# Attention block of eight cores: the odd cores' sums of exponentials by ones matmuls of 32 columns in groups of four, and VectorE's part handed over five steps into the next block

## The reference

```python
q = (x @ Wq).reshape(B, T, H, Dh)            # k and v alike; x here is layernorm(x)
scores = jnp.einsum('bthd,bshd->bhts', q, k)
scores = scores * jnp.tril(jnp.ones((T, T)))  # masked scores are 0, not minus infinity
attn = jax.nn.softmax(scores / T ** 0.5, axis=-1)
out = jnp.einsum('bhts,bshd->bthd', attn, v).reshape(B, T, H * Dh) @ Wo
x = x + layernorm(out)
g = jnp.einsum('th,ih->ti', xf, gate_w) * gate_s   # xf = layernorm(x), INTER = 5632
u = jnp.einsum('th,ih->ti', xf, up_w) * up_s
out = jnp.einsum('ti,hi->th', jax.nn.silu(g) * u, down_w) * down_s
x = x + layernorm(out)
```

## Time and profile before

| | |
|---|---|
| median of 3 runs | 3783.23 us (3782.91 to 4057.18) |
| profiled execution | 3785.3 us, span 3783.8 us on core 7, the slowest |
| odd cores' spans (1, 3, 5, 7) | 3778.8, 3769.3, 3779.7, 3783.8 us |
| even cores' spans (0, 2, 4, 6) | 3709.4, 3714.5, 3705.3, 3709.6 us |
| core 7 busy: TensorE, VectorE, ScalarE | 3685.2, 1424.9, 1158.5 us |
| core 7, span | 3783.8 us = phase A to 1000, B to 1958, W to 2167, C to the end |

### The profile page before, as it was taken

How to read it: one execution, slowest core, us unless ns; L and a number is a source line. 1 busy time by engine, 2 the same in 40 slices (tenths; PEclk the granted TensorE clock), 3 DMA queues, 4 the chain that set the end, 5 groups by cost and what they waited for, 6 DMA issues and landing times.

```text
span 3783.8 us, 50455 instructions; the slowest of 8 cores (3705.3 to 3783.8 us)
## 1 busy us (share of the span) xinstructions
PE 3685.2 (97%) x19252; PEld 1840.7 (49%) x19252; DVE 1424.9 (38%) x1860; ACT 1158.5 (31%) x1511; POOL 173.1 (5%) x235
## 2 busy tenths in 40 slices
PE   6999889999999999999999999999999999999998
PEld 3554444444454555545544444444444456645654
DVE  4641001101389999999976611102111121111112
ACT  2330000000288888888863310000010001101100
POOL 0000000000010000100000000000200001002000
PEclk9999989999999999999999999999999999999999
DMA  7534767798544335353036564554745547666665
GB/s 197 173 123 105 117 124 129 125 134 131 84 62 94 92 78 112 77 106 82 29 134 222 176 209 156 183 173 111 239 156 184 178 145 273 232 212 222 235 201 178
DMA packets 140788, 566.57 MB, mean 150 GB/s; under 512 B 38016, under 2 KB 83200, under 8 KB 111360
## 3 DMA queue, kind: packets, MB, share of 16 engines
q1 hardware_dynamic: 59520, 381.70, 29.6%
q0 software_dynamic: 11440, 125.83, 20.5%
q10 hardware_dynamic: 69584, 55.72, 4.9%
HBM read 595.73 MB, written 147.85 MB: 197 GB/s over the span
## 4 chain that ended last, share of the span: by engine, by line
PE 94%; ACT 2%; DMA 1%; issue 1%; ACTq 1%; DVE 1%; another core or an unknown queue 0%; DVEq 0%; POOL 0%; POOLq 0%; SPq 0%
PE ps L335 93%; ACT pt L369 1%; PE ps L340 1%; ACTq L331 1%; DMA xst<-x 0%; DMA indf<-ind 0%; DVE bna L361 0%; DVE zad L358 0%; ACT rz L369 0%; DMA kscr<-stg 0%; ACT xy L369 0%; DVE xy L360 0%; ACT zst L368 0%; DVE xn L359 0%
## 5 line engine op out<-in xcount | busy, mean ns | idle before, releaser
L335 PE MATMUL ps<-zt,slab 128*128 128x512 bf16 (+1 forms) x5632 | 1069.0, 353 | 6.2 <-DVE xy L360 6.2
L335 PEld LDWEIGHTS ps<-zt,slab 128*128 128x128 bf16 x5632 | 551.7, 98 | 522.4 <-issue 9.9
L369 ACT ACTIVATE pt<-ps 128x1024 bf16<-128x1024 f32 (+2 forms) x752 | 724.9, 981 | 132.9 <-PE ps L335 103.5
L358 DVE TENSOR_TENSOR zad<-zad,pt 128x1024 f32<-128x1024 f32 (+5 forms) x640 | 614.6, 975 | 59.5 <-POOL pt L364 2.9
L335 PE MATMUL ps<-dp,hall 128*128 128x512 bf16 x2332 | 504.0, 379 | 0.0
L360 DVE SCALAR_TENSOR_TENSOR hall<-ps,us_sb,sg 128x512 bf16<-128x512 f32 (+1 forms) x176 | 120.3, 684 | 902.6 <-PE ps L335 902.6
L335 PE MATMUL ps<-qh,kh 128*128 128x512 bf16 (+1 forms) x1760 | 432.4, 339 | 9.8 <-ACT qh L368 5.8
L335 PE MATMUL ps<-pt,vh 128*128 128x512 bf16 (+1 forms) x1760 | 432.3, 339 | 1.8 <-ACT pt L369 1.1
L369 ACT ACTIVATE sg<-ps,gs_sb 128x512 f32<-128x512 f32 (+1 forms) x176 | 111.2, 635 | 878.1 <-PE ps L335 878.0
L357 DVE CAST stg<-ps 128x512 bf16<-128x512 f32 (+1 forms) x136 | 89.7, 660 | 743.0 <-PE ps L335 707.4
L335 PEld LDWEIGHTS ps<-dp,hall 128*128 128x128 bf16 x2332 | 228.2, 98 | 274.9
(11 more groups left out here) (80 smaller groups left out, 1904.8 us busy)
## 6 DMA issues: line engine op xcount, KB each, us to landing
slab<-gwc SPq DMA_DIRECT2D x44, 2048.0 KB, 8.7
slab<-uwc SPq DMA_DIRECT2D x44, 2048.0 KB, 9.5
dp<-dwc SPq DMA_DIRECT2D x165, 512.0 KB, 4.8
xst<-x SPq DMA_DIRECT2D x32, 1024.0 KB, 5.8
gwc<-gw POOLq DMA_DIRECT2D x11, 2048.0 KB, 21.7
uwc<-uw POOLq DMA_DIRECT2D x11, 2048.0 KB, 19.5
dwc<-dw POOLq DMA_DIRECT2D x8, 2816.0 KB, 22.2
kh<-kscr SPq DMA_DIRECT2D x16, 1024.0 KB, 20.0
```

The costliest lines, as they stand in the source:

```text
L335: return c.r.op("tensor", lambda E: E.matmul(out, lhsT, rhs, start=start, stop=stop), waits=waits, inc="pe" if inc else None)
L358: "tt": lambda E, o, a, b, op: E.tensor_tensor(o, a, b, op),
L369: "act": lambda E, o, i, f, **kw: E.activation(o, i, f, **kw),
```

## The change

On the odd cores the units summed by TensorE become 2, 4, 4, 2. Their matmuls are not made step by step any more but all together after the block's last `pv` (`zcols`): the stationary operand is a 128 x 32 matrix of 1/32, and part i of the block's parts goes to the 32 columns of the array and the 32 partitions of bank 6 that start at 32 * (i % 4). VectorE's fold goes to a tile of its own, `zr`, so that `zad` can be started anew; `split`, at the step of the last `pv`, adds bank 6 to `zr` and then makes `zhi` and `zlo`. `zbc` starts bank 6 anew and comes 5 steps after the last `pv` instead of 3. On all cores: `r.split()` stands ahead of ScalarE's first Ln, four casts (two on the even cores) are spread over the V units of g = 1 where two stood at its end, and the first gate and up matmuls of phase C take the ring's two free banks first (`first_banks`).

```diff
@@ Side(1)
-            self.npe = {18: 2, 22: 3, 26: 3, 30: 2}
-            self.lag = {18: 3, 22: 3, 26: 3, 30: 3}
+            self.npe = {18: 2, 22: 4, 26: 4, 30: 2}
+            self.cols = True
+            self.lag = {18: 5, 22: 5, 26: 5, 30: 5}
@@ phase_a
+    ev_w["v0"] = dma(c, "gpsimd", "qw0", c.wres[0][:], d["wv"].ap()[0])
+    r.split()
+
     sop(c, "act", c.lva[1][:], c.eps[:], AF.Ln, waits=[ev_const])
...
     apply(0)
-    r.split()
...
         for cc in range(nch):
-            if g > 1 and cc % 2 == 1:
+            if cc % 2 == 1:
                 next_cast(c, [r.mark("pe")])
...
-            next_cast(c, [r.mark("pe")])
-            next_cast(c, [r.mark("pe")])
@@ phase_b
+    def zcols(bi, us):
+
+        W = width[blocks[bi][1]]
+        parts = [(s, p[2]) for s in us for p in steps[s][4][0]]
+        assert len(parts) % 4 == 0
+        for i, (s, pc) in enumerate(parts):
+            j = i % 4
+            ev_zmm[s] = r.op("tensor", lambda E, j=j, s=s, pc=pc, i=i: E.matmul(
+                bank(c, 6)[32 * j:32 * j + 32, 0:W], c.ones32[:], c.pt[s % NPT][:, pc:pc + W],
+                start=(i < 4), stop=(i >= len(parts) - 4), tile_position=(0, 32 * j)),
+                waits=[ev_sel[s], ev_lnread[bi - 1] if bi >= 1 else c.ev_vs],
+                inc="pe" if i == len(parts) - 1 or parts[i + 1][0] != s else None)
...
+    def split(bi):
+
+        W = width[blocks[bi][1]]
+        Z, e = c.zad, ev_fold[bi]
+        if sd.cols:
+            Z = c.zr
+            u = end_unit[bi]
+            e = vop(c, "tt", Z[:, 0:W], Z[:, 0:W], bank(c, 6)[:, 0:W], ALU.add, waits=[e, ev_zmm[u]])
...
-    mean = (sum(2 * passes(s) + (passes(s) if by_pe(s) else 0) for s in range(per_head))
+    share = 0.25 if sd.cols else 1.0
+    end_unit = {steps[s][0]: s for s in range(N)}
+    mean = (sum(2 * passes(s) + (share * passes(s) if by_pe(s) else 0) for s in range(per_head))
...
+        for p in pv_at.get(s, ()):
+            if sd.cols and steps[p][5]:
+                split(steps[p][0])
@@ phase_c
+    last = [c.ring(L, ds) for ds in range(4)]
+    free = [b for b in range(6) if b not in last]
+    first_banks = (free + last[:2], last[2:] + [6, 7])
...
+            gb, ub = first_banks if b == 0 and ig == 0 else plain
```

More of the change, by code:

```diff
@@ L171, in build_nc @@
     sh.onesb = small("onesb", [128, 128], BF16)
+    sh.ones32 = small("ones32", [128, 32], BF16)
     sh.ebig = small("ebig", [128, 160], BF16)
@@ L936, in zbc @@
         zb = bank(c, 6)[:, 0:W]
-        mm(c, zb, c.onesb[:], c.zhi[:, 0:W], start=False, stop=False, waits=[ev_zlo[bi]])
+        mm(c, zb, c.onesb[:], c.zhi[:, 0:W], start=sd.cols, stop=False, waits=[ev_zlo[bi]])
         ev_zbc[bi] = mm(c, zb, c.onesb[:], c.zlo[:, 0:W], start=False, stop=True, inc=True)
@@ L968, in combine @@
         while half >= W:
-            e = vop(c, "tt", Z[:, 0:half], Z[:, 0:half], Z[:, half:2 * half], ALU.add,
-                    waits=[r.mark("dve")])
+            o = c.zr if sd.cols and half == W else Z
+            w = [r.mark("dve")]
+            ev_fold[bi] = vop(c, "tt", o[:, 0:half], Z[:, 0:half], Z[:, half:2 * half], ALU.add, waits=w)
             half //= 2
+    def split(bi):
+        W = width[blocks[bi][1]]
+        Z, e = c.zad, ev_fold[bi]
+        if sd.cols:
+            Z = c.zr
+            u = end_unit[bi]
+            e = vop(c, "tt", Z[:, 0:W], Z[:, 0:W], bank(c, 6)[:, 0:W], ALU.add, waits=[e, ev_zmm[u]])
         w = [e] + [ev_zbc[b] for b in (bi - 1, bi - 2) if b in ev_zbc]
@@ L1027, in phase_b @@
             if by_pe(p) and not all_pe[steps[p][2]]:
-                zmm(p)
-                work += passes(p)
+                if not sd.cols:
+                    zmm(p)
+                    work += passes(p)
+                elif steps[p][5]:
+                    b = steps[p][0]
+                    us = [q for q in range(p - 8, p + 1) if q >= 0 and steps[q][0] == b and by_pe(q)]
+                    zcols(b, us)
+                    work += share * sum(passes(q) for q in us)
         for p in z_at.get(s, ()):
@@ L1053, in phase_b @@
                 combine(steps[s][0])
+                if not sd.cols:
+                    split(steps[s][0])
+        for p in pv_at.get(s, ()):
+            if sd.cols and steps[p][5]:
+                split(steps[p][0])
     while c.casts:
@@ L1336, in phase_c @@
                     w += slot_free(2)
-                ev_silu[jj] = sop(c, "act", c.sg[jj][:, 0:W], bank(c, jj)[:, 0:W], AF.Silu,
+                ev_silu[jj] = sop(c, "act", c.sg[jj][:, 0:W], bank(c, gb[jj])[:, 0:W], AF.Silu,
                                   scale=c.gs2[:, it:it + 1], waits=w)
-                ev_bank[jj] = ev_silu[jj]
+                ev_bank[gb[jj]] = ev_silu[jj]
             ev_slab_done[k] = e
@@ L1351, in phase_c @@
                     if j == 0:
-                        w = [ev_slab[k + 1], ev_bank[4 + jj]]
-                    e = mm(c, bank(c, 4 + jj)[:, 0:W],
+                        w = [ev_slab[k + 1], ev_bank[ub[jj]]]
+                    e = mm(c, bank(c, ub[jj])[:, 0:W],
                            c.slab[(k + 1) % 3][:, j * 512 + jj * 128:j * 512 + (jj + 1) * 128],
@@ L1357, in phase_c @@
                 it = ig * 4 + jj
-                ev_h[it] = vop(c, "stt", c.hall[:, it * W:(it + 1) * W], bank(c, 4 + jj)[:, 0:W],
+                ev_h[it] = vop(c, "stt", c.hall[:, it * W:(it + 1) * W], bank(c, ub[jj])[:, 0:W],
                                c.us2[:, it:it + 1], c.sg[jj][:, 0:W], ALU.mult, ALU.mult,
```

16 lines of the change are left out of this document (9 added, 7 removed).

## The result

The changed kernel takes 0.9939 times the time of the kernel before, 95% interval 0.9915 to 0.9963: 3759 to 3764 us against 3783 to 3789. It is faster by 0.6%, some 23 us, which is less than the 2% that count as a difference here; the 3727 us and the range of 3700 to 3756 us were wrong. In the profiled execution of the changed kernel die 0 ran at a disturbed clock, so that its rows are read from core 7, on the other die.

The account below looks back on a forecast made before the run. VectorE was taken to bind attention, with TensorE close. Casts 31.6, start 6, attention 11, less 0.4, phase C 8.0 made 56 us off core 7's 3785.3: 3729, as median 3727 us; own range 3714 to 3748, 80% range 3700 to 3756.

Parts of the forecast that it names:

- The casts: Phase A: spreading the casts removes TensorE's 29.9 us wait for stg and the low clock behind it; gain 31.6 us.
- The start: Start of the kernel: the earlier split removes VectorE's idle time and short waits of TensorE; gain 6 us, bounds 3 and 9.
- Phase C: Start of phase C: gate matmuls need not wait for xy; 6.2 + 2.9 gained, 1.1 comes back, net 8.0 us.
- Attention: Sixteen heads on core 7: the new split of sums gains 0.7 us a head, 11 us in all.
- VectorE sets the pace, with TensorE close to it: Attention: VectorE binds, read off the last head's block 26; TensorE's 2.2 us a head less work can't be had.
- The hand-over five steps later: Ends of attention blocks: delaying zbc, lnexp and mul costs nothing, except 0.4 us behind the very last block.
- A head of 58.1 us: Sign in the profile after: attention heads of about 58.1 us, with VectorE still at 0.1 us between its instructions.
- The small matmuls overlap: Attention sums: four 32-column matmuls run at once; the rival without overlap (0.07) lost 27 us, 3765 us.
- the stores didn't starve TensorE: Phase A rival (0.12): the store queue never empties between 391 and 446 us and the stall returns; 3736 to 3747 us.
- The drain rival: Attention: by the skill's rule the new additions pay in full, VectorE loses 0.2 us a head; 3741 us, chance 0.08.
- TensorE alone: Rival: TensorE alone binds attention, each head falls 2.2 us, 35 us instead of 11; 3703 us, chance 0.12.
- heads over 58.9 us: Sign of being wrong in attention: the small matmuls don't overlap, or the new addition waits for them.

Follow-up runs that it names:

- old_casts: old_attention with the casts placed as in the kernel before (none over the V units of g = 1, two at its end); 3774.4 us.
- old_attention: Changed kernel with the attention of the kernel before (units 2, 3, 3, 2, old step-by-step sums, lag 3), all else as changed; 3744.1 us, ratio 0.9884 to before.
- old_banks: old_attention with phase C's first gate and up matmuls in banks 0 to 3 and 4 to 7 again; 3747.1 us, ratio 0.9896 to before.
- second_scores: old_attention with the scores of the fourth unit in each block made twice on the odd cores; head 60.47 us against 58.77.
- second_mul: old_attention with each product with 1/z on the odd cores made twice; head 61.10 us against 58.77.
- capped_fill: Changed kernel, lag 5, at most three q projection matmuls in a step and one in the step with zbc; ratio 0.9906 to before, head 59.23 us.
- spread_units: Changed kernel, but in blocks 22 and 26 TensorE sums the 6th, 5th, 2nd and 1st unit from the end, in two groups; ratio 0.9943 to before.
- pt11: Changed kernel with eleven pt buffers on the odd cores in place of seven; ratio 0.9992 to before, head 59.72 us.
- mixed_lags: Changed kernel with lag 4, 4, 3, 4 for blocks 18, 22, 26, 30 in place of 5; 3732.5 us, ratio 0.9860 to before, head 57.82 us.

## Why the prediction was wrong

Point by point, by its own steps. On core 7 the sum was 56.2 us, and 26.3 came: 3.5 from the start (6 forecast), 34.3 from there to head 0's block 30 (31.6), 15.7 lost in the 15 heads of attention (11 gained), 4.2 won behind them (7.6). The range of the forecast itself adds up to 3751 us at its upper end by the bounds it names, and not to 3748; the result lies outside either.

**The casts, 31.6 us.** Right. No stall between 310 and 450, and the clock full there. From the load of `wk` (rows below) to head 0's block 30 the changed kernel needs 732.2 us and the one before 766.5; from the third load of `wv` to the third of `wk`, where the stall lay, 110.7 against 141.3, 30.6 less. Old_casts puts the latter at 143.4, 32.7 more than old_attention. The 31.0 above is smaller than the whole of its effect, 36.4, because that execution happened to start 5.5 us earlier. The stores did get slower (median of the seven of 512 KB to `vscr` between 290 and 500 us: 20.7 us to landing, 4.1 before), but nobody waited for them.

**The start, 6 us.** Too high, as far as can be told. Up to the load of `wk` for g = 1 all kernels with the earlier split have the same instructions. It is issued on core 7 before, in the changed kernel, in old_attention and in old_casts at

```profile
297.90 0.53 POOL L331 DMA_DIRECT2D wres<-wk  x1 [20.27 <-DVE stg L357]
...
294.35 0.53 POOL L338 DMA_DIRECT2D wres<-wk  x1 [20.27 <-PE ps L342]
...
297.02 0.53 POOL L338 DMA_DIRECT2D wres<-wk  x1 [20.27 <-PE ps L342]
...
291.56 0.53 POOL L338 DMA_DIRECT2D wres<-wk  x1 [20.27 <-DVE stg L364]
```

That is 3.5 us gained in the changed kernel and 0.9 to 6.3 in the same code elsewhere, 3.3 in the middle of the seventeen traces. Block 30 of head 0 in old_casts, 7.4 us earlier than before, looks like the forecast, but that is mostly the luckiest of these starts. There is one trace of the kernel before, and no run undid the earlier split alone. Of the waits it named, those for `xn` stayed (21.6 us in one against 20.8 in three, the first of them 4.5 longer), and that for `wv` shrank by nearly as much (3.6 against 8.0).

**Phase C, 8.0 us.** The mechanism was right, the size wrong: 1.7 us by the rows of old_banks, some 4 in the changed kernel itself. The wait and the clock that go were sized well (8.2 for 9.1). What comes back was put at 1.1 us and was 6.5 in old_attention, 5.0 in the changed kernel. It took `zn` to end at a fixed distance and forgot two things. ScalarE issues the store of `xy` to `yscr` ahead of the `rsb` that `zn` needs, and that issue takes 6.67 us there against 4.67 before; so `zn` ended 17.0 us (2143.35 + 1.34 - 2127.70) behind the transposes instead of 15.0 (2181.63 - 2166.64). And a wait that takes the place of another can bring its low clock along too: here it did behind 3.44 us, and in old_casts, behind 1.75 us, it did not (94 matmuls in 20.45 us).

**Attention, 11 us gained.** This is the wrong step: 16 us were lost, so it is 27 of the 30 us between 3727 and core 7's 3757.5. Start and phase C fell 6 us short, and the casts gave 3 more than forecast. Two sentences of it failed, and something was left out.

"VectorE sets the pace, with TensorE close to it": half right. It was read off the last head, where block 26 was 1.2 us shorter without 3.8 us of TensorE's work. That shows who is next when TensorE's load is gone, not that TensorE doesn't bind when it is there. second_scores shows that it did (1.70 us more for 8 widths of 0.215), and second_mul that VectorE did nearly so. Two engines at their limit mean that load on either costs in full and relief of one is worth little. Of the 2.2 us by which TensorE's work was to fall it said that they can't be had; 1.8 came (58.6 to 56.8 us a head, the waits taken off), and TensorE's waits ate them.

"The hand-over five steps later ... costs nothing": this is the step that cost the time. The same work with lags 4, 4, 3, 4 takes 57.82 us a head; with 5 59.77, and TensorE's waits, 0.95 and 2.94, make the difference. It was examined only for what waits for `zbc`, `lnexp` and `mul`. What it did was to put `zbc` into the step in which the credit hands out four q matmuls, and `lnexp` behind a hole in ScalarE's work. For block 26 capped_fill shows that; for block 30 it is read off the timelines, with a late `mul` at its end (0.59 us). What block 18 loses has the same look, TensorE's 0.70 us wait for exponentials behind `lnexp`, but no run tests it.

Left out was that VectorE might wait for the next block's exponentials: 2.4 us a head. (The wait that it did weigh, of the addition for TensorE's group, "is covered" as it said.) That this is an effect of the above and no cause is shown by spread_units, where there is more of it and no gain, by pt11, and by mixed_lags, where it falls to 3.2 us in the 479.2 without an edit to the units. Nor does it cost 0.4 us behind the very last block: from the first matmul of block 30 in the last head to its `zbc` it takes 12.4 us before and after.

The prices of single instructions were good. VectorE's busy time fell by 0.6 us a head; the forecast's 0.55 had 0.35 of that kind, and 0.20 for two gaps. A head of 58.1 us was forecast, and the right lags give 57.8, but that is near it by luck: it is reached by TensorE's work and waits, 56.9 + 0.95, and not by VectorE's as forecast. The additions of bank 6 start before their forerunners end, as the timeline of `mul` had promised: 1247.20 us against 1246.06 + 1.22 = 1247.28. The prediction set the Trainium skill (VectorE: DVE Perf Modes, The DRAIN you can't avoid) against this, by which the next instruction waits for an empty pipeline. It left out how that paragraph ends: "A next op that is not held starts earlier". The row, 0.08 us early, is no exception to the section as a whole.

**The rivals.** None of them is what happened. The small matmuls overlap, and the stores didn't starve TensorE. The drain rival, 3741 us by 0.2 us a head of VectorE's work, had the right sign for attention and the wrong cause and size. Nearest was TensorE alone (0.12): with the new sums its stream does make up the head, but with waits in it that the rival had not. The sign named for being wrong, heads over 58.9 us, was seen; neither of the two reasons given for it there, no overlap or an addition that waits, was the cause.

## What to carry to other kernels

Where two engines are both near their limit, a move of work from one to the other is worth little; add a known load to each in turn, and the time tells which binds and in which block, before anything is moved. To find where a loop's time went, take the pace-setter's waits off it: if the rest stays the same from version to version, the waits are what to work on. In a software pipeline, where each step mixes work for different stages, the step into which an instruction falls can be worth more than its length: look at the sum of widths step by step in the written order, and at what the next engine has to do behind the widest. When a wait is taken away, follow what is due next with its own queue, the issues of stores on it too.
